# Attention and expert layers on one core: the passes of four engines' programs become loops with a register counter, and the top-k picks move into the first three passes

## The reference

```
xn  = layernorm(x)
q, k, val = xn @ Wq + bq, xn @ Wk + bk, xn @ Wv + bv       # 16 heads of 16 values
pos = sinusoid(512, 256) @ Wp + bp
score = (einsum(q + u, k) + relative_shift(einsum(q + v, pos))) / sqrt(16)
attn  = softmax(score) @ val, heads side by side, @ Wo + bo
# experts: 8 experts, each batch sends its 128 best tokens to each expert
probs = softmax(xn @ gate_w);  g, m = top_k(probs per expert, 128)
h = gelu(xn[m] @ w1) @ w2;  ffn = scatter_add(g * h)       # rounded to bfloat16
out = x + attn + ffn
```

## Time and profile before

| | us |
|---|---|
| median of 3 runs | 4877.9 |
| lowest and highest | 4870.25, 4880.08 |
| the profiled execution, its own time | 4870.25 |
| its span, from first to last instruction | 4868.3 |
| PE busy | 4764.4 (98%) |
| DVE busy | 3686.6 (76%) |
| ACT busy | 3460.6 (71%) |
| POOL busy | 1710.5 (35%) |

### The profile page before, as it was taken

One profiled execution on the slowest core, in us unless ns is written; L12 is line 12 of the kernel. 1 busy time (PEld: TensorE's weight loads), 2 busy tenths in 40 slices (PEclk: granted clock), 3 DMA queues, 4 the chain that ended last, 5 costly groups with the idle time before them and its releaser, 6 DMA issues. The chain is left out here.

```text
span 4868.3 us, 111786 instructions
## 1 busy us (share of the span) xinstructions
PE 4764.4 (98%) x42412; PEld 3658.5 (75%) x42412; DVE 3686.6 (76%) x8040; ACT 3460.6 (71%) x5180; POOL 1710.5 (35%) x1545
## 2 busy tenths in 40 slices
PE   7899999999999999999999999989999999999997
PEld 3477777777777777777777777769999999999997
DVE  7699999999999999999999989963555555533344
ACT  3689989999998998999889999954333333344454
POOL 0222322222232222223222222224656565644443
PEclk9899999999999999999999999999999999999999
DMA  9899999999999999999999999973545555433259
GB/s 353 323 369 366 369 372 366 370 370 367 370 367 371 363 373 367 373 357 378 367 370 370 368 370 366 365 280 83 127 116 136 132 120 134 105 62 84 45 154 317
DMA packets 394026, 1389.58 MB, mean 285 GB/s; under 512 B 51104, under 2 KB 128800, under 8 KB 327712
## 3 DMA queue, kind: packets, MB, share of 16 engines
q1 hardware_dynamic: 270624, 778.39, 44.0%
q0 software_dynamic: 122880, 604.05, 38.7%
HBM read 708.00 MB, written 674.23 MB: 284 GB/s over the span
## 5 line engine op out<-in xcount | busy, mean ns | idle before, releaser
L735 DVE CUSTOM_DVE_ANT_0 att_shifted<-att_quad,att_shifted 128x512 f32<-128x512 f32 x2048 | 1324.1, 684 | 88.7 <-PE att_quad L977 88.4
L599 ACT ACTIVATE att_shifted<-att_shifted,att_mn 128x512 f32<-128x512 f32 x2048 | 1360.6, 717 | 0.3 <-DVE att_mn L735 0.3
L594 ACT ACTIVATE ring<-att_quad 128x1024 f32<-128x1024 f32 x1024 | 1047.8, 1023 | 308.6 <-PE att_quad L965 308.4
L998 PE MATMUL att_tp<-ident,att_shifted 128*128 128x128 f32 x8192 | 1122.5, 280 | 6.1 <-DVE att_pt L745 5.3
L745 DVE COPY att_pt<-att_tp 128x512 f32<-128x512 f32 x1536 | 1011.0, 686 | 128.9 <-PE att_tp L998 121.3
L998 PEld LDWEIGHTS att_tp<-ident,att_shifted 128*128 128x128 f32 x8192 | 878.8, 141 | 301.6 <-issue 175.2
L1461 DVE TENSOR_TENSOR ffn_hp<-ring,ffn_hp 128x512 fp32r<-128x512 f32 x512 | 477.7, 933 | 685.8 <-ACT ring L1398 662.6
L485 POOL DMA_DIRECT2D att_shifted<-xs_d x512 | 279.3, 545 | 2038.0 <-DMA xs_d<-ring 1691.7
L1396 ACT ACTIVATE ffn_hp<-ffn_up 128x512 fp32r<-128x512 f32 x512 | 305.9, 597 | 915.0 <-PE ffn_up L1542 899.8
L965 PE MATMUL att_quad<-att_pos,att_qv 64*128 64x512 f32 x2048 | 832.3, 447 | 12.0 <-ACT ring L594 11.9
L1503 PE MATMUL ffn_yp<-ffn_w2p,ffn_hp 128*128 128x256 f32 x6144 | 827.7, 284 | 3.4 <-DVE ffn_hp L1461 1.7
(11 more groups left out here) (111 smaller groups left out, 4694.5 us busy)
## 6 DMA issues: line engine op xcount, KB each, us to landing
xs_d<-ring SPq DMA_DIRECT2D x1024, 513.0 KB, 8.2
att_shifted<-xs_d POOLq DMA_DIRECT2D x512, 1024.0 KB, 9.3
att_shifted<-in_L_attn_x_dram SPq DMA_DIRECT2D x32, 512.0 KB, 7.0
xn_d<-att_shifted SPq DMA_DIRECT2D x32, 512.0 KB, 6.4
xt_d<-att_shifted SPq DMA_DIRECT2D x32, 512.0 KB, 7.6
gathered<-xt_d SPq DMA_DIRECT2D x32, 512.0 KB, 11.0
att_d<-att_osb SPq DMA_DIRECT2D x512, 32.0 KB
ring<-in_L_ffn_w_dram SPq DMA_DIRECT2D x16, 1024.0 KB
```

Of the source, the lines that this page charges most:

```text
L594: act.activation(xo[:, kk % NW, 2 * half:2 * half + 2, 1:S + 1], xp[:, :, :], ACT.Copy).then_inc(x_out, 1)
L599: act.activation(shifted[:, kk % NX, t], shifted[:, kk % NX, t], ACT.Exp, bias=mn[:, kk % NX, t:t + 1], scale=-1.0).then_inc(exp_done, 1)
L735: dve.tensor_tensor_reduce(out=shifted[:, kk % NX, t], in0=sp_[:, t % 2], in1=shifted[:, kk % NX, t], scale=-0.25, scalar=-NEG, op0=ALU.ad ...
L998: ins = pe.transpose(tp[:, c % 2, t * P:(t + 1) * P], shifted[:, kk % NX, t, c * P:(c + 1) * P], ident[:, :])
```

## The change

- `first_apart` and `ends_apart` are new; `ends_apart(eng, n, body)` runs pass 0 with a number, passes 1 to 14 as a loop whose counter is in a register (`Fori`), and pass 15 with a number. SP, POOL and ACT use it for the 16 attention passes. (`first_apart` is not called.)
- DVE and PE run passes 0, 1 and 2 written out, passes 3 to 14 as a loop, and pass 15 written out.
- The picks now stand in passes 0 to 2 (`EARLY = 3`), five in every four heads from the second head on: `range(5 * (n - 1) // 4, 5 * n // 4)`. The 96th has been made after 77 heads, and the lists are kept in pass 2.
- In the expert phase SP, ACT, DVE and PE run experts 0 and 1 written out, 2 to 4 as a loop, 5 and 6 as another, and 7 written out. POOL's program stays as it was.

```diff
@@ new helpers @@
+def ends_apart(eng, n, body):
+
+    body(0)
+    with eng.Fori(1, n - 1) as i:
+        body(i)
+    body(n - 1)
@@ attention_phase @@
-    PICK_EVERY = 4
-    LISTS_AT = 12
+    EARLY = 3
...
         def picks_at(i, kk):
 
-            n = i * BH + kk
-            return (n // PICK_EVERY,) if n % PICK_EVERY == PICK_EVERY - 1 else ()
+            n = i * BH + kk if isinstance(i, int) and i < EARLY else 0
+            return range(5 * (n - 1) // 4, 5 * n // 4) if n else ()
 
         def lists_at(i, kk):
-            return i == LISTS_AT and kk == H + 1
+            return isinstance(i, int) and i == EARLY - 1 and kk == H + 1
...
@@ SP, POOL and ACT, each @@
-                for i in range(ITERS):
-                    body(i)
+                ends_apart(sp, ITERS, body)
...
@@ DVE and PE, each @@
-                for i in range(ITERS):
+                for i in range(EARLY):
                     body(i)
+                with dve.Fori(EARLY, ITERS - 1) as i:
+                    body(i)
+                body(ITERS - 1)
...
@@ ffn_phase; called as experts(sp, body), and so for ACT, DVE and PE @@
-        def experts(body):
-
-            for e in range(NE):
-                body(e, mixing=MIX <= e < MIX + B // NG)
+        def experts(eng, body):
+
+            body(0)
+            body(MIX)
+            with eng.Fori(MIX + 1, MIX + B // NG) as e:
+                body(e, mixing=True)
+            with eng.Fori(MIX + B // NG, NE - 1) as e:
+                body(e)
+            body(NE - 1)
...
@@ SP's body in the expert phase @@
-                            if not (e == MIX and g == 0):
+                            if not (isinstance(e, int) and g == 0):
                                 store_mid(b - 1, (g - 1) % 2)
```

More of the change, by code:

```diff
@@ L53, in wait_alone, with first_apart @@
         eng.nop(nofuse=True)
+def first_apart(eng, n, body):
+    body(0)
+    with eng.Fori(1, n) as i:
+        body(i)
[4 more added lines that the diff above has]
+    body(n - 1)
 class Shared:
@@ L517, in body @@
                             with_v(i, t + 1)
-                for i in range(ITERS):
-                    body(i)
+                ends_apart(pool, ITERS, body)
                 pool.wait_ge(picked, 2)
@@ L655, in body @@
                             o_evacuate(i, kk // QH - 1)
-                for i in range(ITERS):
-                    body(i)
+                ends_apart(act, ITERS, body)
                 for t in range(1, TT):
@@ L1128, in body @@
                             ins.then_inc(back, 1)
-                for i in range(ITERS):
+                for i in range(EARLY):
                     body(i)
+                with pe.Fori(EARLY, ITERS - 1) as i:
+                    body(i)
+                body(ITERS - 1)
                 times_values(ITERS, -LAG - 1)
@@ L1313, in body @@
                             store_out(g)
-                experts(body)
+                experts(sp, body)
                 for n in range(2):
@@ L1410, in _ @@
                 split_x(0, 0)
-                experts(body)
+                experts(act, body)
                 for g in (NG - 2, NG - 1):
@@ L1482, in _ @@
                 split_x(0, 0)
-                experts(body)
+                experts(dve, body)
                 for k in range(GB):
@@ L1552, in _ @@
                 turn(0, 0)
-                experts(body)
+                experts(pe, body)
                 for k in range(GB):
```

## The result

The changed kernel takes 5004.19 us (median of 4 runs, 5003.01 to 5017.39), the kernel before 4875.3 us (4 runs, 4870.25 to 4880.08): a ratio of 1.0265, with an interval of 1.0249 to 1.028. The forecast was 4981 us and slower; it was right in sign and 23 us short. The profiled execution has a span of 5003.4 us where the one before had 4868.3, 135.1 us more: 128.2 us of them in attention (the last add ends at 3333.4 instead of 3205.2 us), 6.9 us in the expert phase.

What follows compares the result with a forecast made beforehand. PE was taken to bound the expert phase and be first of four nearly full engines in attention. Terms 20 + 55 + 6 + 19 + 3 = 103 us gave 4973 us profiled, 4981 us against the median; 8-in-10 range 4900 to 5110.

Steps and rivals of the forecast that it cites:

- What bounds the kernel: Attention: PE full, DVE and ACT nearly so, so stops are paid fully or nearly; PE alone bounds the expert phase.
- The picks, 20 us: Passes 0 to 2: DVE becomes the bound at 6.14 us a head over 77 heads, 20 us; later passes gain nothing.
- The jumps, 55 + 6 us: Attention's pass ends: code fetch stops of 4 us, 11 jumps at 5 us, plus 6 us for two without PE and DVE.
- the factor of 1.25: Attention's jumps: engines' stops mostly lie side by side but not quite, counted as 1.25 stops of 4 us a pass.
- The register instructions, 19 us: PE's looped attention: one exposed instruction of 50 ns a head over 384 heads, 19 us; ends 0 and 200 us.
- The rival of dear registers: Looped attention heads: register instructions cost 0.3 us a head instead of 0.05, 96 us more, 5077 us; chance 0.18.
- The expert phase, 3 us: Expert loops: three jumps back, stops mostly hidden, 1 us of each, 3 us; ends 0 and 33 us.
- The sign of at most 5 us there: Expert phase: what would show the forecast is a phase as long as before within 5 us.
- Jumps that are nearly free: Pass ends: code is kept or fetched before queued work ends; only picks, registers and a rest stay, 4913 us; chance 0.15.
- 15 us for the registers and a rest: Whole kernel: what the rival of nearly free jumps added to the picks' 20 us to reach 4913 us; chance 0.15.
- Less code fetched: Looped attention: bodies stay on chip and DMA engines set the pace, up to 14 us won, 4864 us; chance 0.03.

Runs made afterwards that it cites:

- the unrolled ones: Changed kernel with every loop written out again, only the picks moved into passes 0 to 2: 4878.34 us, ratio 1.0021 to the kernel before.
- ACT, moved: Unrolled kernel with only ACT's attention looped, its loop's first instruction placed at the start of a block of code: 4958.5 us, ratio 1.0165.
- all, ACT moved: Changed kernel, all queues looped, with ACT's loop head alone at the first place of a block of code: 4979.59 us, ratio 1.0211.
- PE, half load: Kernel with only PE's attention looped, and from pass 4 on half the rows of the shift stored and loaded: 4910.58 us, ratio 1.0096.
- the two passes in a body: Changed kernel with two passes written out in each attention body, 5 jumps of PE and DVE, 6 of the others: 4947.92 us, ratio 1.0144.
- announced jumps: Changed kernel with its loops' jumps announced at the head of each pass: 4907 us, ratio 1.008; with ACT's loop head also moved 4912.6 us, 1.0104.

## Why the prediction was right or wrong

Most of the pass ends' price can be put together from the trace: PE's idle gaps of more than 1.5 us, and half of its busy time at a clock of 0.50. Beside it stands what the pass ends were longer than the unrolled ones (us, summed over the jumps).

```
looped       jumps  PE idle  half of slow work  sum   pass ends longer by
all            13     67.9        40.2          108        113
PE             11     50.3        25.6           76         75
ACT            13     93.9        34.0          128        130
DVE            11     40.9        20.5           61         65
ACT, moved     13     38.8        29.9           69         71
all, ACT moved 13     47.5        26.8           74         76
PE, half load  11     22.9        11.5           34         35
```

**What bounds the kernel.** Right: PE is full in attention, and a stop of any of the three engines is paid nearly whole. The rows of ACT and DVE looped alone show it; their slack of 0.4 to 0.6 us a head covered little.

**The picks, 20 us.** 16.8 us in passes 0 to 2, with heads of 6.13 us where 6.14 was worked out, 2.4 us of which comes back later. The prediction had put that return at nothing.

**The jumps, 55 + 6 us.** The step that failed in size, with the mechanism right: the pass ends cost 113 us, 52 more than forecast: 96 where all engines jump (55 forecast), and 7.1 and 10.1 at the ends of passes 1 and 2, where only ACT, POOL and SP jump (6 forecast). Three things were missing. The stop was taken as 4 us, near a 64 KB load in the prelude, which did not meet full DMA engines (a share of 0.61 in the first 5 us); PE's branch took 6.1 us at the median, and 3.8 only where the traffic was halved. The term counted one fetch for each jump; ACT needed two, and when its loop head was moved the pass ends became 37 us shorter. And the term took a stop as idle time alone; PE's clock fell behind it, which cost 40 us of the 113. I had the row for the clock before me, 1.00 in every stretch, and asked what idle time would add, but not what it would do to the work behind it. That the stops lie side by side was right: PE, DVE and ACT looped alone cost 75, 65 and 130 us at the pass ends, 270 if added up, and looped together they cost 113. What the factor of 1.25 for their not being quite in step should have been is not told apart from the three.

The page "Runtime: NRT & Kernel Launch" of the Trainium skill, section "Instruction fetch mechanics", which the prediction weighed, has the rule that decided: a taken branch out of the code held stops the engine until it has come. The trace agrees, with 83 ns for a branch that isn't taken and 6.1 us for one that is.

**The register instructions, 19 us.** They cost nothing that shows. Each takes 29 to 53 ns on PE's sequencer, but heads inside looped passes take 5.888 us where the unrolled ones take 5.899, with PE looped alone and, at the median, with all looped. The lower end of that term was zero; it should have been taken, since two thirds of PE's issue time was known to be free. The rival of dear registers is refuted by that, and by the two passes in a body.

**The expert phase, 3 us.** It cost 6.9 us in the changed kernel and 8.0 when looped alone: that is 2.3 and 2.7 us paid of each stop of 3.8 us, where 1 us had been counted. The sign of at most 5 us there was missed.

**The other rivals.** Jumps that are nearly free needed code that is kept or comes in time. Only POOL's did. With announced jumps the time came near to that rival's 4913 us, at 4907. (Its 15 us for the registers and a rest do not fit the 19 us that the sum has for the registers alone.) Less code fetched fails twice: the packets rose from 350 and 172 to 385 and 314, and attention was not bound by transfers, as the half load shows.

**The sum by measured terms.** 17 - 2 for the picks, 113 for the pass ends, -3 for the shorter looped heads, 7 for the experts: 132 of the 135 us between the profiled executions. Of the rest, 1.4 us lie ahead of the first add and 1.2 us in the last pass. That the forecast was only 23 us short is in part luck: the jumps were put 52 us too low, the registers 22 us too high.

Shown by experiments: that the jumps' code fetch is the cost (announced, halved in number), that ACT's double stop is two blocks (moved head), that the fetch's length hangs on the traffic (half load). Worked out from traces and not isolated by a run of its own: the clock's 40 us, and what the traffic lengthens within a fetch.

## What to carry to other kernels

A loop around a long body saves no code traffic and costs a stop of several microseconds at each jump back on every engine that is nearly full; price it with the length of the DMA queues at that place, count the blocks that the loop head touches, and write out or announce the jumps where the bound engine has no slack. Announced jumps had their stop where the loop was left, here some 6 us once. Where PE is the bound, price a stop as its idle time plus the half-speed work behind it. Register arithmetic beside matmuls and adds as long as these can be taken as free until a trace says otherwise.

## What the hardware showed that I had not expected

- The same branch takes 6.1 to 6.3 us at a DMA share of 0.97 to 0.99 and 3.8 us at 0.47 to 0.60.
- A loop head near the end of a block of code doubled ACT's stop: 4.69 us, one activation, 4.36 us. Placed at a block's start, one stop of 4.79 us.
- POOL's loop of 228 instructions never stopped (0.25 us from the branch to the next instruction), twice that length stopped for 4.4 to 5.6 us each time.
- A double stop of ACT alone, 13 times, costs more at the pass ends than the stops of all five queues together: 130 and 113 us.
- The load changes the wait before a code packet and not the packet: 3.4 to 5.2 us under full traffic, 0.9 to 1.6 us under half, with packets of 0.9 to 1.4 us in both.
- An announced jump that isn't taken has a stop: ACT 5.9 to 6.0 us and DVE 4.4 to 4.6 us where the attention loop was left, in both kernels with announced jumps.
- PE's granted clock fell to 0.50 after idle times of 2.5 to 7 us at all of the changed kernel's pass ends, and stayed there for 3.4 to 10.2 us by its records; after idle times of about 1.8 us it fell at some and not at others.
- A looped head is 0.011 us shorter than a written-out one on PE (5.888 to 5.899 us). Why was not tried.
